# Batch 0's row maxima from float32 scores on row groups of 32 partitions, before the stacked operands have come back from memory

## What is computed

```
q1, q2, k, v = x @ Wq1, x @ Wq2, x @ Wk, x @ Wv      # 16 heads of 16 features
scores = einsum('bhqd,bhkd->bhqk', [q1; q2], [k, k]) * 0.25
scores = where(causal, scores, min)
p = softmax(scores);  y = p @ v
y = y1 - sigmoid(x @ Wlam) * y2
x = layernorm(x + y @ Wo)
x = layernorm(x + ffn(x))
```

## Time and profile before

| what | value |
|---|---|
| median of three runs | 478.38 us (477.83 to 478.87) |
| span of the profiled execution, first to last instruction | 475.2 us |
| TensorE busy | 418.3 us, 88% of the span |
| VectorE, ScalarE, GpSimd busy | 281.4, 237.2, 244.9 us |
| mean granted TensorE clock | 0.962 of full speed |

### The profile page before, as it was taken

How to read it: one execution, slowest core, us unless ns; L and a number is a source line. 1 busy time by engine, 2 the same in 40 slices (tenths; PEclk the granted TensorE clock), 3 DMA queues, 4 the chain that set the end, 5 groups by cost and what they waited for, 6 DMA issues and landing times.

```text
span 475.2 us, 10336 instructions
## 1 busy us (share of the span) xinstructions
PE 418.3 (88%) x4008; PEld 335.1 (71%) x4008; DVE 281.4 (59%) x676; ACT 237.2 (50%) x532; POOL 244.9 (52%) x334
## 2 busy tenths in 40 slices
PE   4138688899999999999999999999999999998995
PEld 4126237675897669874998579875988578855995
DVE  3627138743758366745858366745757477836474
ACT  4604472458253844577254844476355841484240
POOL 8305384547254745657254845567364831384142
PEclk9859599889999999999999999999999999999999
DMA  8762760444023710371123510370024510000000
GB/s 288 242 147 78 196 175 1 122 128 99 3 58 97 171 46 13 111 174 32 46 78 102 146 46 26 100 197 30 23 82 103 121 46 1 4 1 24 1 23 23
DMA packets 34753, 40.41 MB, mean 85 GB/s; under 512 B 4240, under 2 KB 28304, under 8 KB 34448
## 3 DMA queue, kind: packets, MB, share of 16 engines
q1 hardware_dynamic: 34704, 39.75, 30.5%
HBM read 27.94 MB, written 11.53 MB: 83 GB/s over the span
## 4 chain that ended last, share of the span: by engine, by line
PE 66%; DVE 12%; ACT 11%; issue 4%; DMA 3%; SPq 2%; POOL 1%; POOLq 0%; DVEq 0%; ACTq 0%
PE ff L668 10%; PE ff L670 9%; PE ff L669 9%; ACT prob L514 7%; PE ybank L780 7%; DVE neg_max L1013 6%; PE ring L731 5%; PE ring L752 4%; PE ybank L668 3%; PE ybank L793 3%; PE ybank L670 3%; PE ybank L669 3%; PE ring L726 3%; PE ring L756 3%; ACT h_hi L474 2%
## 5 line engine op out<-in xcount | busy, mean ns | idle before, releaser
L1013 DVE TENSOR_REDUCE neg_max<-ring 128x2 f32<-128x512 f32 (+3 forms) x176 | 104.3, 638 | 44.3 <-PE ring L731 43.6
L514 ACT ACTIVATE prob<-ring 128x512 f32<-128x512 f32 x192 | 100.3, 619 | 14.8 <-PE ring L752 14.7
L399 POOL TENSOR_TENSOR h_lo<-h_full,h_hi 128x256 fp32r<-128x256 f32 x72 | 53.1, 737 | 101.1 <-ACT h_hi L474 101.1
L409 POOL TENSOR_SCALAR_AFFINE_SELECT prob<-prob 128x512 f32<-128x512 f32 x128 | 83.5, 677 | 23.8 <-ACT prob L514 23.5
L668 PE MATMUL ff<-x1T_hi,wg_lo 128*128 128x256 f32 x288 | 86.4, 300 | 0.2
L669 PE MATMUL ff<-x1T_lo,wg_hi 128*128 128x256 f32 x288 | 80.8, 281 | 0.0
L670 PE MATMUL ff<-x1T_hi,wg_hi 128*128 128x256 f32 x288 | 80.7, 280 | 0.0
L1034 DVE COPY yv<-ybank 128x256 f32<-128x256 f32 x64 | 26.5, 422 | 75.5 <-PE ybank L780 75.5
L522 ACT ACTIVATE gate_t<-ff 128x256 f32<-128x256 f32 x72 | 27.9, 387 | 75.1 <-PE ff L670 74.1
L726 PE MATMUL ring<-mask_b,ident_b 128*128 128x128 bf16 (+2 forms) x176 | 45.1, 256 | 18.9 <-DMA q_stack<-qk_parts_dram 17.3
L731 PE MATMUL ring<-k_stack,q_stack 96*128 96x256 bf16 (+3 forms) x512 | 60.1, 239 | 0.0
(11 more groups left out here) (164 smaller groups left out, 892.4 us busy)
## 6 DMA issues: line engine op xcount, KB each, us to landing
q_stack<-qk_parts_dram SPq DMA_DIRECT2D x48, 256.0 KB, 4.6
qk_parts_dram<-parts SPq DMA_DIRECT2D x72, 128.0 KB
k_stack<-qk_parts_dram SPq DMA_DIRECT2D x48, 128.0 KB, 4.4
xt_raw<-xT SPq DMA_DIRECT2D x8, 256.0 KB, 2.8
xz<-x SPq DMA_DIRECT2D x8, 256.0 KB, 2.9
out<-xz SPq DMA_DIRECT2D x7, 256.0 KB, 2.2
prob<-w_gu SPq DMA_DIRECT2D x1, 1152.0 KB, 7.3
yv<-w_gu SPq DMA_DIRECT2D x1, 1024.0 KB, 9.3
```

Source lines behind the costliest of these rows:

```text
L399: pool.tensor_tensor(h_lo[:, n, :], h_full[:, n % RING, :], h_hi[:, n, :].bitcast(F32), ALU.subtract).then_inc(h_lo_done, 1)
L409: pool.affine_select(out=v, in_=v, compare_op=ALU.is_ge, fill=0.0, base=0, pattern=[[0, 2], [HALF, 2], [0, 2], [1, HALF]], channel_multipl ...
L514: act.activation(prob[:, g % RING, u, :], ring[u][:, :], ACT.Exp, scale=SCALE).then_inc(exp_done, 1)
L1013: dve.tensor_reduce(neg_max[:, columns.start:columns.stop, i], ring[u % RING][:, 0:len(columns) * keys].rearrange("p (h k) -> p h k", k=keys),
```

## The change

Batch 0's max pass no longer uses the stacks. ScalarE copies the projected queries out of PSUM as float32 (`first_query`, into `q_first`) and the keys twice (`first_keys`, into `k_first`), once with the odd and once with the even heads multiplied by zero through a per-partition scale (`parity`). A row group of 32 partitions holds two heads of 16 features, so a float32 matmul over those 32 partitions with the masked keys gives the scores of one head. `first_pair` fills two banks at a time from two different row groups, alternating between them matmul by matmul, in the banks `ff0`, `ff1` and `ring0`, `misc` in turn; `first_max` reduces them in 24 units. The values' projection follows pair 1, batch 1's projections follow pairs 3, 5 and 7.

Around it the start is laid out anew. SyncE loads only the first gate/up piece and batch 1's `xT` before batch 0's stores, the other two pieces after the stacks, and stores batch 1's parts after batch 0's maxima. The low part of the first gate/up piece moves from VectorE to GpSimd (counted by `prob_raw_done`), ahead of GpSimd's split of batch 1's `xT`. The output and router weights' low parts and gate/up pieces 2 and 3 are split behind the max pass. The stacks are awaited only by the second pass.

```
+FIRST_TILE_HEADS = (4, 4, 2, 2)
+FIRST_JOBS = tuple((i, g * FIRST_HEADS + j * heads, heads) for i, heads in enumerate(FIRST_TILE_HEADS)
+                   for j in range(FIRST_HEADS // heads) for g in range(P // ROW_GROUP))
...
+FIRST_V_AT, FIRST_QK_AT = 1, (3, 5, 7)
...
+        first_banks = ((ff[0], ff[1]), (ring[0], misc))
...
         @block.sync
...
+            load_gate_up(0)
+            load_xt(1)
             for n, p in ((0, 0), (1, 0), (0, 1), (2, 0), (1, 1), (2, 1), (0, 2), (1, 2), (2, 2)):
                 store_part(0, n, p)
-            load_xt(1)
             load_stacks(0)
+            for n in range(1, len(GU_PIECES)):
+                load_gate_up(n)
...
         @block.gpsimd
...
             for n in range(QK_JOBS):
                 third_part(0, n)
+            k, cols, raw = GU_PIECES[0]
+            split_weight(1, wg_lo[:, k, cols], raw, wg_hi[:, k, cols], prob_raw_done)
...
         @block.scalar
...
+            def first_query(n):
+                act.wait_ge(qk_full, n + 1)
+                copy(q_first[:, n, :].rearrange("p (i h t) -> p h i t", h=2, i=Q_TILES), psum_order(qk_bank(0, n)[:, :])).then_inc(q_first_done, 1)
+
+            def first_keys():
+                act.wait_ge(qk_full, QK_JOBS)
+                act.wait_ge(parity_made, PARITIES)
+                for x in range(PARITIES):
+                    act.activation(k_first[:, x, :, :], qk_bank(0, QK_JOBS - 1)[:, :].rearrange("p (n t) -> p n t", n=KEY_BLOCKS), ACT.Copy,
+                                   scale=parity[:, x:x + 1]).then_inc(k_first_done, 1)
...
         @block.tensor
...
+            def first_pair(n):
+                pair = range(2 * n, 2 * n + 2)
+                if n == 0:
+                    pe.wait_ge(q_first_done, Q_JOBS)
+                    pe.wait_ge(k_first_done, PARITIES)
+                elif n == 1:
+                    pe.wait_ge(qk_h_done, QK_JOBS)
+                    pe.wait_ge(qk_rest_done, QK_JOBS)
+                else:
+                    pe.wait_ge(max_done, 2 * n - 2)
+                for u in pair:
...
+                    pe.matmul(o[:, :, keys - HALF:keys], ident_b[:, :], mask_b[:, :].unsqueeze(1).to_broadcast([P, heads, HALF]),
+                              start=True, stop=False, skip_group_check=True)
...
+                for j in range(heads):
+                    for u in pair:
+                        row, block = spot(FIRST_JOBS[u][1] + j)
+                        rows = slice(row // 2 * ROW_GROUP, (row // 2 + 1) * ROW_GROUP)
+                        mm = pe.matmul(first_bank(u)[:, j * keys:(j + 1) * keys], q_first[rows, block, i * P:(i + 1) * P],
+                                       k_first[rows, row % PARITIES, block, 0:keys], start=False, stop=True, skip_group_check=True)
...
+                for n in range(0 if has_prev else FIRST_PAIRS):
+                    first_pair(n)
+                    if n == FIRST_V_AT:
...
+                        for t in range(TT):
+                            v_job(0, t)
+                    if n in FIRST_QK_AT:
+                        qk_job(1, FIRST_QK_AT.index(n))
```

More of the change, by code:

```diff
@@ L49 @@
 CONSTS = 6
+PARITIES = 2
 ROUTER_STEPS = 5
@@ L300, in iteration @@
                 load_max(i)
+                if is_first(i):
+                    sp.wait_ge(stack_loaded, 16 * STACK_LOADS)
+                    store_parts(i + 1, range(QK_JOBS))
                 if has_next:
@@ L342, in _ @@
             pool.memset(minus_half[:, :], -0.5).then_inc(const_step, 1)
[L343 to L346, removed]
+            pool.wait_ge(const_step, 5)
             for h in range(2):
@@ L638, in _ @@
                 split_weight(wp_hi[:, :, proj_chunk(c)], wp_raw[:, :, proj_chunk(c)], wp_loaded[c])
-                if c > 0:
-                    first_part(0, c - 1)
+            first_query(0)
+            first_part(0, 0)
             split_weight(wp_hi[:, :, proj_chunk(QK_JOBS)], wp_raw[:, :, proj_chunk(QK_JOBS)], wp_loaded[QK_JOBS])
-            second_part(0, 0)
+            first_query(1)
+            first_part(0, 1)
+            first_keys()
             first_part(0, QK_JOBS - 1)
-            for n in range(1, QK_JOBS):
+            for n in range(QK_JOBS):
                 second_part(0, n)
@@ L950, in _ @@
                 qk_job(0, n)
-            pe.wait_ge(w_hi_done, W_PROJ)
-            pe.wait_ge(w_lo_done, W_PROJ)
-            for t in range(TT):
-                v_job(0, t)
-            pe.wait_ge(consts_made, CONSTS)
+            pe.wait_ge(consts_made, CONSTS - 1)
             for i in range(B):
@@ L1015, in row_max, with first_max, make_parity @@
                                   negate=True).then_inc(max_done, 1)
+            def first_max(u):
+                dve.wait_ge(s_full, u + 1)
+                i, first, heads = FIRST_JOBS[u]
+                keys = (i + 1) * HALF
+                dve.tensor_reduce(neg_max[:, first:first + heads, i], first_bank(u)[:, 0:heads * keys].rearrange("p (h k) -> p h k", k=keys),
+                                  AX_X, ALU.max,
+                                  negate=True).then_inc(max_done, 1)
+            def make_parity():
+                dve.wait_ge(consts_made, 2)
+                for x in range(PARITIES):
+                    dve.tensor_reduce(parity[:, x:x + 1], ident[:, :].rearrange("p (g x d) -> p x g d", x=PARITIES, d=HEAD_DIM)[:, x, :, :],
+                                      AXES_XY, ALU.add).then_inc(parity_made, 1)
             def max_second(b):
@@ L1145, in iteration @@
                 if not has_prev:
-                    for u in range(SEAM_UNITS):
-                        row_max(i, u)
+                    for u in range(FIRST_UNITS):
+                        first_max(u)
                 else:
                     norm_mean(0, *before)
-                for u in range(SEAM_UNITS, S_UNITS):
+                for u in range(SEAM_UNITS, S_UNITS if has_prev else SEAM_UNITS):
                     row_max(i, u)
@@ L1160, in iteration @@
                 max_second(i)
+                if not has_prev:
+                    split_weight(W_OUT, wo_lo[:, :, :], wo_raw, wo_hi[:, :, :])
+                    split_weight(W_ROUTER, wr_lo[:, :, :], wr_raw, wr_hi[:, :, :])
+                    for n, (k, cols, raw) in enumerate(GU_PIECES[1:]):
+                        split_mlp_weight(n + 2, wg_lo[:, k, cols], raw, wg_hi[:, k, cols])
+                    dve.wait_ge(v_done, TT)
                 attn[0](dve.tensor_scalar(lam[:, :, :], lam_th[:, :, :], 0.5, 0.5, ALU.mult, ALU.add))
```

112 lines of the change are left out of this document (74 added, 38 removed).

## The result

The changed kernel is slower: 483.5 us as the median of four runs (481.56 to 490.07) against 478.62 (477.83 to 479.43) for the kernel before, a ratio of 1.0098 [1.0069, 1.0127]. Forecast were 473.5 us, and the time lies outside the range. The ratios leave disturbed runs out (one of the four here), so a ratio can differ from that of the two medians.

What follows compares the result with a forecast made beforehand. It took batch 0's start chain to be the bound, with TensorE idle from 14.3 to 31.4 us. The max pass ends 4.9 us earlier, the rest stays hidden: 478.38 - 4.9 = 473.5 us, range 469.5 to 480.7.

Steps and rivals of the forecast that it cites:

- Pair 1 ends at 16.8, the 12 value matmuls behind it at 18.3: TensorE, batch 0's max pass: times in us for the second score pair and value projections, ahead of ScalarE's value copies.
- the 4.9 us: Batch 0's max pass: predicted to end 4.9 us earlier, at 43.6 instead of 48.48, all of it shortening the span.
- the wait for `xt_lo`: TensorE ahead of batch 1's first projection: held for GpSimd's low part of batch 1's x, from about 21 to 27.5.
- `wg_hi`: ScalarE behind the values' copies: high part of gate/up piece 1, predicted 2.14 us, ending at 21.0.
- the subtraction: GpSimd's low part of gate/up piece 1, 2304 columns: predicted 5.1 us, ending at 26.1.
- so the down weights are issued where they were before: SyncE behind batch 0's maxima: 21 issues instead of 12 from 45.4 on, third down piece issued at 59.3.
- The row groups run abreast: TensorE's float32 score pairs: two row groups overlap, 0.79 us (pairs 4 to 7) or 1.05 (8 to 11) before masks.
- rival in part abreast: TensorE's score pairs: row groups overlap only partly, pairs cost 1.15 and 1.49 us, 2.9 us won, 475.5; chance 0.14.
- From the wait's end to the end of the max pass: Batch 0's max pass after TensorE's restart at 27.5: projections and pairs 4 to 11, ending at 43.6.
- The 3.5 us to the second pass: Batch 0, from transposed maxima to the second pass's start: predicted to stay 3.5 us.
- VectorE's four subtractions: VectorE behind batch 0's maxima: 3072 columns, some 4 us, hidden ahead of its first product copy in the second pass.
- The place of the wait: TensorE's predicted standstill in batch 1's first projection, behind pair 3, some 6.5 us of the old hole.

Runs made afterwards that it cites:

- e11: Changed kernel plus 12 overwritten filling matmuls ahead of pair 0 and 14 behind it; ratio 1.0103 to the kernel before.
- the run with all moves and fills: Changed kernel with batch 1's stores, value projections, values' copies and batch 1's x split moved earlier, plus 14 filling matmuls after pair 0; 471.97 us, ratio 0.9868.
- E3: Changed kernel with only the value projections moved ahead of pair 0 on TensorE, late stores kept; 477.21 us, ratio 0.9952 to the kernel before.
- e9: Changed kernel with batch 1's stores again ahead of batch 0's maxima and value projections ahead of pair 0; 474.88 us, ratio 0.991 to the kernel before.
- e4: Changed kernel with each pair's matmuls issued bank by bank instead of alternating between row groups; one run, 488.44 us.
- e5: Changed kernel with batch 1's stores, value projections, values' copies and batch 1's x split all moved earlier, no fills; 470.86 us, ratio 0.9851.
- e2: Changed kernel with batch 1's x split right behind the values, its low part ahead of GpSimd's gate/up subtraction, late stores kept; 476.46 us, ratio 0.9896.
- the two edits together: All-moves kernel with 14 filling matmuls and batch 0's maxima issued after six of batch 1's nine stores; 466.87 us, ratio 0.9763 to the kernel before.

## Why the prediction was wrong, point by point

**The step "Pair 1 ends at 16.8, the 12 value matmuls behind it at 18.3" failed, and with it the 4.9 us.** It priced both at full clock. The row had shown the clock still at full 3.8 us after the last matmul, and I took that hold for granted across the two short waits; the runs show it falling 0.4 us into pair 1 (0.92 over 14 to 18, so from about 17.4 on). Pair 1 started at 17.0 instead of 16.0 (bank 2 was copied at 12.50, not 11.8, the rest ended at 16.87), took 2.2 us instead of 0.8, the values 2.9 instead of 1.5: 1.0 + 1.4 + 1.4 = 3.8, which is what the wait for `xt_lo` ended late by (31.26 against 27.5). The run with fills in the changed kernel (e11) tells the clock's share: there the clock held, pair 1 took 1.36 us and the values 1.60, and the wait ended at 28.68 (pair 1 also began 0.4 us earlier). So some 2.1 of the 3.8 us are the clock, 1.0 is the late start, and 0.7 was priced too low at any clock: a record of 64 columns takes the same step as one of 128 (0.11 us each at full clock in the run with all moves and fills). Everything on the chain behind had its predicted size: `wg_hi` 2.12 (2.14), the subtraction 5.05 (5.1), `xt_lo` 1.26 (1.29). E3 and e9, which take the values out from behind pair 1 and run them at full clock, bear the chain out: the wait ends at 26.0 and 26.4 and the maxima come at 43.1 and 43.8.

**The step "so the down weights are issued where they were before" failed too.** It counted 21 issues and no wait between stores and stack loads. SyncE waits there until the stores have landed, and from the first store to the third down piece went 17.1 us (50.18 to 67.29) instead of 13.9 (45.4 to 59.3); 2.5 of the 3.2 us are that wait. So the 4.9 us could not have got through even if the max pass had ended as predicted: with the first store at 45.4 the piece is issued at 62.5, lands 7.0 later, is split by 70.3, and the values' copy comes 3.6 us ahead of 73.89, not 4.9. E3 shows it with a max pass that ended near the predicted time: 3.5 us ahead. In the changed kernel the copy came 1.1 late, and batch 1's maxima 1.4 late, behind matmuls at half clock. That a DMA's semaphore has its full count only when all of its data has landed is what the Trainium skill says ("DMA: Bandwidth & Descriptors", "Why a DMA increments its semaphore by 16 and not by 1"). The trace agrees, with 2.5 us from the end of the last store's issue (50.18 + 5.71) to the first stack load at 58.42, which starts when the stores have landed (53.94 + 4.46).

**What was right.** The row groups run abreast; a pair costs 1.06 us (192 columns) and 1.28 (256) at full clock, against 0.91 and 1.17 predicted and 1.15 and 1.49 of the rival in part abreast, so the price was a little low and the first of the two lies nearer to the rival. From the wait's end to the end of the max pass went 16.9 us (predicted 16.1), with the clock rising again 3.1 us after the restart (0.58 over 31 to 35, so at 34.4; predicted 4.7); that the sum nearly met is in part luck, since an earlier clock and dearer pairs offset each other. The 3.5 us to the second pass stayed, and VectorE's four subtractions, done at 53.4, had 4.25 us to spare before its next copy. The place of the wait was right; only its end was not.

**Open.** Between the maxima of batch 1 and batch 7 the changed kernel loses another 1.3 us (1.4 to 2.75), and 1.8 more behind that, where the clock is 0.58 between 444 and 448 and 1.00 in the kernel before, with 23 matmuls against 37 in those 4 us. No experiment says why the clock falls there, and runs of one kernel differ in such falls. Nor is it settled how long the clock stays at half after a pause: 3.1 us behind the restart in the changed kernel, 16 in e4, and 10 in e5 from where it fell, all under unbroken work. And e2 with its late stores has runs as fast as e9's median and faster, which the account above does not explain.

## What to carry to other kernels

Price every matmul that follows a pause at both clock levels, even where the pause is as short as the 1.45 and 1.69 us here, and ask what a chain costs if it lands in the slow one: here a delay of 3.8 us, 2.1 of them the clock's, ate most of a gain of 4.9, and 12 matmuls moved ahead of the pauses gave it back. When a store is moved on an in-order queue, count its landing and everything behind the load that needs it, not only its issues; the stores' new place cost 5.5 us, more than the max pass was to win. After each edit look again for what waits: the fills won 4.5 us that two small loads behind nine stores took, and the two edits together won what neither won alone.

## What the runs showed that was not expected

- Two row groups run abreast even when their matmuls stand bank by bank in the program (starts 0.01 us apart with two heads a bank, 0.92 with four). The Trainium skill ("TensorE: Matmul & The Clock Gate", Part 3) has matmuls start in strict program order. The rows of e4 differ: `misc`'s first record at 37.41 is 0.47 us ahead of `ring`'s second at 37.88, which stands before it in the program.
- A record of a float32 row-group matmul takes the same step with 64 columns as with 128: 0.21 us at half clock, 0.11 at full.
- 14 overwritten matmuls in a pause of 1.7 us kept the clock at full through 14 to 35 us, of which some 10 us ran at half clock without them.
